# Top-k attention keys: one-hot gathering products replaced by row numbers and indirect transfers

## The reference

```python
scores  = (x @ Ws.T + bs).transpose(0, 2, 1)        # one score per sequence, head, token
top_idx = jax.lax.top_k(scores, 128)[1]             # the 128 best of 512 tokens
k_t, v_t = gather(k), gather(v)                     # their keys and values, per head
attn_t  = einsum('bhnd,bhkd->bhnk', q, k_t) * scale
topk_out = einsum('bhnk,bhkd->bhnd', softmax(attn_t), v_t)
```

## Time and profile before

| | |
|---|---|
| device time, 3 runs | median 569.43 us (568.0 to 571.01) |
| span of the profiled execution | 567.5 us; no separate time of this execution is given beside it |
| PE / DVE / ACT / POOL busy | 497.0 / 390.0 / 350.9 / 311.3 us |
| instructions | 13117 |
| stages | to 97, to 147, to 169, to 483, to 567.5 us |
| group loop, from one output copy to the next (ACT L1126) | 15.1 to 25.7 us a group, many between 18.2 and 19.2 |

### The profile page before, as it was taken

How to read it: one execution, slowest core, us unless ns; L and a number is a source line. 1 busy time by engine, 2 the same in 40 slices (tenths; PEclk the granted TensorE clock), 3 DMA queues, 4 the chain that set the end, 5 groups by cost and what they waited for, 6 DMA issues and landing times.

```text
span 567.5 us, 13117 instructions
## 1 busy us (share of the span) xinstructions
PE 497.0 (88%) x4267; PEld 307.3 (54%) x4267; DVE 390.0 (69%) x1400; ACT 350.9 (62%) x835; POOL 311.3 (55%) x464
## 2 busy tenths in 40 slices
PE   7999899886767999999899989899987878789886
PEld 4477676676434445545455545445544422668664
DVE  4777876468886698899878897777975650235325
ACT  6587555786208676667567668566664455567653
POOL 3411165456499976493199967897075051354340
PEclk9999999998989999999999999999999697999999
DMA  7996011764210000000000000010001005356506
GB/s 229 360 362 228 2 42 56 255 206 156 64 29 14 3 14 14 14 4 15 12 9 9 15 12 14 27 30 20 12 4 45 12 34 183 125 183 195 163 15 185
DMA packets 47539, 47.78 MB, mean 84 GB/s; under 512 B 10323, under 2 KB 39129, under 8 KB 47472
## 3 DMA queue, kind: packets, MB, share of 16 engines
q1 hardware_dynamic: 44464, 41.37, 23.2%
q0 software_dynamic: 3008, 5.58, 3.1%
HBM read 11.32 MB, written 19.48 MB: 54 GB/s over the span
## 4 chain that ended last, share of the span: by engine, by line
PE 58%; DVE 17%; issue 9%; ACT 7%; DMA 3%; POOL 3%; another core or an unknown queue 2%; SPq 1%; DVEq 0%; ACTq 0%; POOLq 0%
PE BANK L1836 5%; PE BANK L1935 5%; PE BANK L1912 4%; PE BANK L1804 4%; PE BANK L1792 4%; PE BANK L1884 4%; PE BANK L2022 4%; PE BANK L1941 2%; PE BANK L1938 2%; PE BANK L2160 2%; PE BANK L1741 2%; PE BANK L1907 2%; POOL OH L725 2%; DVE XN_c L1460 2%
## 5 line engine op out<-in xcount | busy, mean ns | idle before, releaser
L1117 ACT ACTIVATE PT<-BANK 128x256 f32<-128x256 f32 (+2 forms) x352 | 158.1, 493 | 108.5 <-PE BANK L1912 75.1
L725 POOL TENSOR_SCALAR OH<-IOTA,POS 128x128 bf16<-128x128 bf16 x240 | 140.1, 604 | 4.3 <-DVE OH L1580 3.2
L1460 DVE CUSTOM_DVE_ANT_0 XN_a<-BANK,BANDQ 128x256 f32<-128x256 f32 (+1 forms) x128 | 56.7, 443 | 25.6 <-PE BANK L1884 15.6
L1460 DVE CUSTOM_DVE_ANT_0 XN_c<-BANK,BANDQ 128x384 f32<-128x384 f32 (+1 forms) x128 | 67.9, 530 | 9.3 <-PE BANK L1884 5.5
L733 POOL TENSOR_TENSOR SUM<-NRM 128x128 f32<-128x128 f32 x16 | 7.3, 456 | 104.5 <-DVE NRM L1481 104.5
L1465 DVE TENSOR_REDUCE QST<-BANK 128x4 f16<-128x512 f32 x64 | 44.2, 694 | 16.8 <-PE BANK L1889 12.7
L1935 PE MATMUL BANK<-PT,V 128*32 128x256 f32 (+1 forms) x512 | 49.1, 456 | 0.7 <-issue 0.3
L757 POOL DMA_INDIRECT yt_late<-QKV,IDY_late x31 | 30.4, 979 | 32.7 <-DVE QKV L1338 25.2
L1836 PE MATMUL BANK<-XNT_ALL,W 128*128 128x512 f32 x96 | 45.3, 596 | 0.0
L934 ACT ACTIVATE PT<-BANK 128x512 f32<-128x512 f32 x48 | 27.6, 598 | 22.3 <-PE BANK L1836 20.4
L1907 PE MATMUL BANK<-BANDK,IDB 128*128 128x256 bf16 x128 | 36.0, 282 | 5.7 <-issue 3.5
(11 more groups left out here) (363 smaller groups left out, 1286.6 us busy)
## 6 DMA issues: line engine op xcount, KB each, us to landing
xs_late<-W SPq DMA_DIRECT2D x1, 6984.0 KB, 38.4
xs_early<-W SPq DMA_DIRECT2D x1, 4680.0 KB, 19.6
KZB<-W SPq DMA_DIRECT2D x16, 256.0 KB
KZC<-W SPq DMA_DIRECT2D x15, 256.0 KB
PT<-W SPq DMA_DIRECT2D x11, 256.0 KB
QKV<-xs_late SPq DMA_DIRECT2D x31, 72.0 KB
W<-w SPq DMA_DIRECT2D x2, 1024.0 KB, 8.5
QKV<-xs_early SPq DMA_DIRECT2D x23, 72.0 KB
```

The costliest lines, as they stand in the source:

```text
L725: last = nc.gpsimd.tensor_scalar(OH[g % 2][:, i, t, :], IOTA[:, :], POS[:, t, c:c + 1], None, ALU.is_equal)
L1117: nc.scalar.activation(PT[u % PT_RING][:, 0:w], P2_BANK[u % SCORE_RING][:, 0:w], ACT.Exp, scale=SCALE).then_inc(S["exp_done"], 1)
L1460: nc.vector.tensor_tensor_reduce(out=JUNK[v % 2][:, 0:n], in0=P1_BANK[v % SCORE_RING][:, 0:n], in1=BANDQ[:, off:off + n], scale=1.0, scala ...
```

## The change

The choice of the top 128 is made differently. The 512 scores of a head are laid as two halves of 256, on different partitions; for each half the 128 best are found with their positions, sorted: `max`, `max_index` and `match_replace` over 64 rows of 256, 47 steps instead of 32. DVE writes both lists forwards and backwards, PE turns them (four turns of 64 by 128), and one comparison of list A with list B backwards gives the 128 best of the two (`row_choice`, 6 DVE operations), as row numbers in `CHOSEN`. Keys (f16 parts, 64 bytes) and values (32 bytes) of each token and head stand as one row of 96 bytes in DRAM (`KV_ROWS`, 786 KB a sequence), written by POOL, ACT and one SP transfer a sequence. POOL reads 128 rows a head with an indirect transfer, 4 a group, copies the parts, and PE turns the keys with one product. The diff, cut to its core:

```diff
-MORE_ROUNDS = {(g, u) for g in range(1, 5) for u in (1, 4, 7, 11, 12, 17, 20)} | {(5, u) for u in (1, 2, 3, 5)}
+MORE_ROUNDS = {(g, u) for g in range(1, 5) for u in range(0, UNITS, 2)} | {(5, u) for u in (0, 2, 4)}
-ROUNDS_TILE = {i: 1 + (i + 1) % 2 if i < 13 else 2 for i in range(4, NT_EARLY - 1)}
-VALUES_TILE = {7: (0, 1), 11: (2,), 15: (3,)}
+ROUNDS_TILE = {i: 2 if i < 12 else 3 for i in range(4, NT_EARLY - 1)}
+ROWS_TILE, STORE_TILE = 7, 12
@@ sync: constants (8 small loads for BS, one more for WS), early tiles, group loop
+                             (KSH[:, :], kshift), (WS[:, SLOT:SLOT + H], w_s[:, 0:H]),
+                             *((BS[r:r + H, :], chan[...]) for r in range(0, P, H))):
+            def store_rows(b):
+                sp.wait_ge(S["kv_ready"], b + 1)
+                sp.dma_start(rows_b, KV[...]).then_inc(S["kv_stored"], 16)
                 tile_load(EARLY, n, read[n % READ])
+                if n == STORE_TILE:
+                    store_rows(0)
@@ for g in range(NG):
+                if g % GROUPS == GROUPS - 1 and g // GROUPS + 1 < B:
+                    store_rows(g // GROUPS + 1)
@@ gpsimd
+            def key_rows(b):
+                pool.wait_ge(S["stack"], b + 1)
+                pool.wait_ge(S["value_hi"], b + 1)
+                nc.gpsimd.tensor_copy(KV[:, :, :, 0:K_W]..., kst).then_inc(S["kv_ready"], 1)
-            def onehot(g, parts=range(HG)):
+            def gather(g):
+                if g % GROUPS == 0:
+                    pool.wait_ge(S["kv_stored"], 16 * (g // GROUPS + 1))
+                if g >= 2:
+                    pool.wait_ge(S["got_k"], g - 1)
+                for i in range(HG):
+                    nc.gpsimd.indirect_dma_start(GOT[g % 2][:, i, :], None, KV_ROWS[g // GROUPS][:, :], ...)
+            def gathered(g):
+                pool.wait_ge(GOT_IN[g % 2], got_done(g))
+                ...
+                nc.gpsimd.tensor_copy(VSEL[g % 3][:, :, PART:PART + DH], GOT[g % 2][:, :, K_W:K_W + DH])
+                nc.gpsimd.tensor_copy(GOT_K[g % 2][:, :, :], GOT[g % 2][:, :, 0:K_W]).then_inc(S["got_k"], 1)
@@ for n in range(NT_EARLY):
                 tile_out(EARLY, n)
-                for part in VALUES_TILE.get(n, ()):
-                    value_part(0, part)
+                if n == ROWS_TILE:
+                    key_rows(0)
@@
             global_values(0)
-            pool.wait_ge(S["onehot_dve"], 1)
-            onehot(1)
+            pool.wait_ge(S["sel_done"], 1)
+            gather(0)
+            gather(1)
             rstd("c", 2)
             rstd("c", 3)
-            onehot(2)
+            gathered(0)
+            gathered(1)
+            gather(2)
@@ for g in range(NG):
-                if g + 3 < NG:
-                    onehot(g + 3)
+                if g + 2 < NG:
+                    gathered(g + 2)
...
+                if g == SEL_GROUP:
+                    pool.wait_ge(S["sel_done"], 2)
+                if g + 3 < NG:
+                    gather(g + 3)
@@ scalar: the value parts now in groups 0, 4, 8, right behind the stack parts, at u == 8
-                        elif g % GROUPS == 1:
                             value_first_parts(b)
@@ vector
-            mask(0)
+            picks(0, PICKS)
+            both_orders(0)
             maxima(range(0, 3))
             dve.wait_ge(S["sel_t"], 1)
-            marks(BANK[0]).then_inc(S["sel_t_s"], 1)
+            row_choice(0, BANK[0], False)
             maxima(range(3, 7))
-            dve.wait_ge(S["sel_pos"], 1)
-            places(0, PLACE_BANK).then_inc(S["sel_done"], 1)
-            ... 16 compares into OH[0] ...
-            maxima(range(7, 10))
-            gathered_kv(0)
             for a in range(EARLY.first, B):
                 add_experts(EARLY, a)
                 ...
-            maxima(range(10, UNITS_Q))
+            maxima(range(7, 14))
+            chosen_keys(0)
+            maxima(range(14, UNITS_Q))
@@ tensor
-            def gather_kv(g):
-                ... 16 products for the keys, 16 for the values
+            def turn_keys(g):
+                pe.wait_ge(S["got_k"], g + 1)
+                pe.wait_ge(S["misc_free"], free("kv", g))
+                nc.tensor.transpose(MISC16[:, 0:K_TOP], chosen, IDH[:, :]).then_inc(S["misc_full"], 1)
-            for w in range(3, 7):
+            for w in range(3, 14):
                 p1(0, w)
-            keep_busy(IDLE_BANK, 2)
-            ... sel_places, units 7 to 9, keep_busy 10, gather_kv(0), keep_busy 8 ...
-            for w in range(10, UNITS_Q):
+                keep_busy(IDLE_BANK, 1)
+            keep_busy(IDLE_BANK, 4)
+            turn_keys(0)
+            keep_busy(IDLE_BANK, 4)
+            for w in range(14, UNITS_Q):
```

More of the change, by code:

```diff
@@ L34 @@
 ROUNDS = K_TOP // 8
+PICKS = 3 * ROUNDS - 1
+REST = 16 * (11 + P // H)
+LH = L // 2
 SLOT = 32
+K_W = SLOT // 2
+KV_W = K_W + DH
 LN_EPS = 1e-5
@@ L405, in build @@
                         *(xb[:, :, :].rearrange("p t d -> p (t d)") for xb in XB), *RELU]
+        KV_ROWS = [nc.dram_tensor(f"kv_rows{b}", [L * H, KV_W], F32) for b in range(B)]
         XS = {w.tag: nc.dram_tensor("xs_" + w.tag, [w.slots, ROW_W], F32) for w in (EARLY, LATE)}
@@ L1405, in _, with picks @@
             taken = [0, 0]
-            def rounds(w, halves):
-                sc, sw, m8 = SC[0:ROWS_SEL, :], SW[0:ROWS_SEL, :], M8[0:ROWS_SEL, :]
-                for n in range(taken[w], taken[w] + halves):
+            def picks(w, count):
+                sc, sw = SC[0:ROWS_SEL, 0:LH], SW[0:ROWS_SEL, 0:LH]
+                for n in range(taken[w], min(taken[w] + count, PICKS)):
+                    k, step = divmod(n, 3)
                     if n == 0 and w:
@@ L1414, in rounds @@
                         dve.wait_ge(S["sel_score_s"], 1)
-                    src = sc if n < 2 else sw
-                    if n % 2 == 0:
-                        link(nc.vector.max(m8, src))
-                    else:
-                        link(nc.vector.match_replace(out=sw, in_to_replace=m8, in_values=src, imm_value=TAKEN))
-                taken[w] += halves
-            def mask(w):
-                assert taken[w] == 2 * ROUNDS
-                nc.vector.tensor_scalar(SC[0:ROWS_SEL, :], SW[0:ROWS_SEL, :], TAKEN, None, ALU.is_equal).then_inc(S["sel_mask"], 1)
@@ new lines, in picks, with both_orders @@
+                    if step == 0:
+                        link(nc.vector.max(best, src))
+                    elif step == 1:
+                        link(nc.vector.max_index(found, best, src))
+                    else:
+                        link(nc.vector.match_replace(out=sw, in_to_replace=best, in_values=src, imm_value=TAKEN))
+                taken[w] = min(taken[w] + count, PICKS)
+            def both_orders(w):
+                assert taken[w] == PICKS
+                best, tseb = BEST[0:ROWS_SEL, :, :], TSEB[0:ROWS_SEL, :, :]
+                link(nc.vector.tensor_copy(best[:, 1, :], FOUND[0:ROWS_SEL, :]))
+                nc.vector.tensor_copy(tseb, best[:, :, ::-1]).then_inc(S["sel_found"], 1)
@@ L1593, in _ @@
                     if (g, u) in MORE_ROUNDS:
-                        rounds(1, 1)
-                        if taken[1] == 2 * ROUNDS:
-                            mask(1)
+                        picks(1, 1)
+                        if taken[1] == PICKS:
+                            both_orders(1)
                     if g == 0 and u == KV_ONE + 1:
-                        gathered_kv(1)
+                        chosen_keys(1)
                     if (g, u) == (7, 1):
@@ L1612, in _ @@
                         dve.wait_ge(S["misc_full"], full("sel"))
-                        marks(MISC).then_inc(S["misc_free"], 1)
-                    if (g, u) == (SEL_GROUP, POS_AT + 1):
-                        dve.wait_ge(S["misc_full"], full("pos"))
-                        places(1, MISC).then_inc(S["misc_free"], 1)
+                        row_choice(1, MISC, True)
                     if (g, u) in GATES:
@@ L2100, in _ @@
                     if g == 0 and u == KV_ONE:
-                        gather_kv(1)
+                        turn_keys(1)
                     kind, *which = C_AT.get((g, u), ("none",))
```

204 lines of the change are left out of this document (91 added, 113 removed).

## The result

The changed kernel took 600.03 us in the median of four runs (596.93 to 601.9), beside 570.22 us for the old one in the same job: a ratio of 1.051, with a 95% interval of 1.046 to 1.056. The forecast was 568.8 us, in a range of 561 to 577. The change is slower here, well outside that range. Jobs came in two kinds, those in which the old kernel takes 568 to 573 us (the first, and two later ones) and those in which it takes 542 to 544, and the runs within a job mostly agree with each other, so that kernels are compared by their ratio to the old one in the same job (one run, 582.8 us of the spread version, lies over 1.5% above the same kernel's other one and is left out).

The account below looks back on a forecast made before the run. TensorE held 58% of the critical chain and bounded most loop groups, with VectorE close. Terms 0 + 3.3 + 5.6 - 10.0, plus 0.5 for a colder TensorE, gave -0.6 us: 568.8 us, range 561 to 577.

Parts of the forecast that it names:

- cost nothing in the loop: Groups' loop: waits for landed rows, read-back stores and indirect reads add 0, covered by about 10 us before the turn.
- Loop: Group loop: one key turn replaces `gather_kv` on TensorE, less value-copy cost; -10.0 us, bounds -6 and -13.
- the 1.3 for the value copies: Groups 0, 4 and 8: ACT's two value copies follow four stack copies, so exponentials queue longer; +1.3 us.
- Group 5: Loop, group 5: picks end earlier, places are gone and the turn saves too; -3.3 us, to under 19.
- Groups 6 to 13: Loop, where TensorE is the bound: 0.77 us saved in each of eight groups, -6.2 us.
- groups 9 to 11: Loop, a sign that the prediction is right: each of these groups 0.8 us shorter.
- rival (c): Early tiles and group 0: TensorE's clock drops after standing, up to 6.2 us lost; 574.5 us, chance 0.28.
- Early tiles: Before the loop: tile 13's load queues behind the new row store, TensorE stands; +3.3 us, bounds 0 and +5.5.
- Choice chain: Key choice before the loop: eight transfer issues and two `rstd` delay the top maxima; +5.6 us, bounds +3 and +8.
- Constants: Before the experts: nine more SP loads, last constant some 5 us later, TensorE not held; 0, bound +1.
- Picks: VectorE's top-128 selection: half-length max, position search and replacement at 0.49 us or less; 47 steps, 22 us against 23.
- (d): Loop: cover for the reads gone, TensorE stands at the key turn, 1 us a group; 583 us, chance 0.03.

Follow-up runs that it names:

- spread version: Changed kernel, most of the loop's indirect transfers set apart and the start reordered: 535.0 us (ratio 0.985); in the slow kind of job 573.3 beside 572.5 old.

## Why the prediction was wrong, point by point

The step that failed is one sentence on the loop: that the gathers themselves "cost nothing in the loop". I priced an indirect transfer at the 1.27 us that it holds GpSimd and asked only whether GpSimd had room. In the first kind of job a row of four reads in the loop holds up the other engines as well, by 0.8 to 2.1 us as measured on ScalarE, and one of eight transfers by 4.4 to 7.6. The rows of the changed kernel lose 26.2 us more than the old one's, and the loop missed its forecast by 24.0 (14.0 more in place of 10.0 less). The start missed by 3.4 (12.3 against 8.9), most of it in the choice of keys. The old trace showed the effect. The 3.07 us of TensorE in the earlier trace rows lie inside a row of eight writes of GpSimd (431.5 to 441.5), and ScalarE stood 3.94 us there with the same "remote" as its cause. I read that row as one on the clock. Had I asked what GpSimd did just then, a price was there to be estimated: group 13 took 25.73 us where its neighbour took 20.84, at a clock of 0.81.

Without that term the sum can be judged in the other kind of job, by the profiled executions of the third job (542.9 us old, 541.2 changed), one run each. Up to the first output copy the change costs 10.1 us (forecast 8.9), in the loop it gains 12.1, and behind the last copy it costs 0.3, together -1.7 (forecast -0.6). That the total is near is in part luck, as single terms miss both ways:
- **Loop**: -10.0 forecast, -12.1 measured (269.9 to 257.8 us between the first and the last output copy). Groups 1 to 3: -0.53, -0.47, -0.52 (forecast -0.45 each). Group 4: +0.16 (forecast -0.45, and a third of the 1.3 for the value copies). Group 5: -5.2 (forecast -3.3; in the first job it was -3.1). In the third job the old kernel had a clock of 0.93 there and took 23.33 us, against 21.78 in the first, so 1.6 of the 5.2 are not the change's doing. Groups 6 to 13: -5.4 in all (forecast -6.2), but not -0.77 each: from -1.93 in group 8 to -0.12 in group 10. So groups 9 to 11 were not each 0.8 shorter (-0.15, -0.12, -0.46); what else held them was not traced. Group 0, forecast at 0, took 1.8 longer, with a clock of 0.50 for 6.8 us from 187.9 in the changed kernel; that is a sign of rival (c), in this job alone.
- **Early tiles**: +3.3 forecast, bounds 0 to +5.5. From the first to the last tile's write: +3.3 in the first job, +4.7 in the third (38.3 to 43.0 us), so the term held. Moving the store alone shortened this stage by 5.2 (42.3 to 37.0 us, fourth job), more than the term, to below the old kernel's 38.3: the wait costs more than I took, and with the store moved the stage is 1.3 shorter than the old one, for a reason that was not traced.
- **Choice chain**: from the last write of the early tiles to ScalarE's copy behind the top maxima 22.2 us before and 26.6 after: +4.5 (forecast +5.6); in the first job it was +8.4 by the end of that write. The eight issues come 1.34 us apart on average in the first job and 1.39 in the third (forecast 1.27).
- **Constants**: 0; the changed kernel's early tiles begin no later (106.2 against 107.0). **Picks**: 0.41 us each, as forecast.
- **Rivals**: (c) priced the clock at 6.2 us. In the loop of the first job the granted clock was 0.50 for 20.4 us in five stretches, against 17.0 in two of the old kernel. Half of the difference is lost at most, so it explains under 2 us of the 27; the longest stretch begins in the standing time of group 9. (d), at 583 us, came nearest to the 600, but by another mechanism: in seven groups of the loop GpSimd waits 1.4 to 1.9 us for the rows, and TensorE never waits for them at the turn of the keys. What costs is how they are issued. The Trainium skill's rule on GpSimd's descriptors (SBUF — State Buffer, the passage on the "DVE blocks DMA" trap) is on VectorE's two-port operations, an fp32 copy within SBUF for one; no stretched issue showed here: the 64 reads' issues took a mean of 1.018 us, 1.187 at most.
- The sum of the prediction, -0.6 us, stands against a ratio of 0.998 (0.995 to 1.002) in the third job, and against 1.051 in the first.

## What to carry to other kernels

Before an indirect transfer by GpSimd is added to a stage whose other engines are full, look in the old trace at what TensorE and ScalarE do during the rows of such transfers that are already there, and price a row by that, not by GpSimd's time alone. Issue them singly (here some 4 us apart lost nothing in most cases), or by SP where the rows are known in advance, and look in the trace whether they did come apart. And run the two kernels together in more than one job: here one job said 5% slower and another no difference.

## What the runs showed that I had not expected

The same program took 541 us in some jobs and 599 in others. It is not the chip by its number: chip 14 gave 541.1 us for the changed kernel in the fourth job and 599.1 in the fifth. In most groups in which GpSimd issues nothing the two kinds agree to 0.1 us, often to 0.01 (17.98 in group 3); the old kernel's group 8 is an exception, with 19.14 in the first job and 19.90 in the third. What makes GpSimd's transfers harmful in one kind of job was not found. One more difference lies in the traces: they hold 7475 semaphore updates of the changed kernel in the first job and 7456 in the fifth, but 10584 in the third and in the fourth. Of the 3109 missing between the first job and the third, 2837 are updates by landing transfers. They are missing where time is lost: for the old kernel's work from 205 to 350 us of the first job, where GpSimd issues no transfer, the lists of both kinds have 1184 landings and 926 other updates each, and for that from 430 to 450, with eight writes, 29 of 154 landings. Whether the loss and the lateness have one cause stays open, and so whether the recording itself takes part in the delay; every execution here was recorded, and a run without records wasn't tried. The Trainium skill (NOTIFIC — Programmer's Manual, When the ring fills) says that a full queue of records drops the new one, writes over the oldest, or stalls the engine that produced it, as it was set up; no run here shows which, if any, holds in either kind of job.
